# Last layer of a four-layer transformer: key and value projections folded into other weights

## The reference, cut to what matters

```python
nx = _layer_norm(x, ln_gamma, ln_beta)
q = nx @ Wq
k = prototype_bank @ Wk            # prototype_bank is the context
v = prototype_bank @ Wv
scores = einsum('bth,bph->btp', q, k) * H ** (-0.5)
weights = softmax(scores, axis=-1)
evidence = einsum('btp,bph->bth', weights, v)
combined = concatenate([nx, evidence, anchor], axis=-1)
router_probs = softmax(combined @ router_W + router_b, axis=-1)
h = silu(einsum('btc,ecr->bter', combined, e_w1) + e_b1)      # 3 experts, r = 256
expert_out = einsum('bter,erh->bteh', h, e_w2) + e_b2
routed = sum(expert_out * router_probs[..., None], axis=-2)
g = sigmoid(silu(combined @ gate_w1 + gate_b1) @ gate_w2 + gate_b2)
return x + g * (routed @ out_w + out_b)
```

## Time and profile before

| | |
|---|---|
| device time, median of 3 runs | 3569.41 us (3560.76 to 3570.86) |
| the profiled execution's own time | 3567.66 us |
| its span, first to last instruction | 3565.9 us |
| busy share of the span | PE 87%, DVE 77%, ACT 64%, PEld 58%, POOL 33% |
| last phase | from 3156.90 us to the end of the span |

### The profile page before, as it was taken

One profiled execution on the slowest core, in us unless ns is written; L12 is line 12 of the kernel. 1 busy time (PEld: TensorE's weight loads), 2 busy tenths in 40 slices (PEclk: granted clock), 3 DMA queues, 4 the chain that ended last, 5 costly groups with the idle time before them and its releaser, 6 DMA issues. The chain is left out here.

```text
span 3565.9 us, 94724 instructions
## 1 busy us (share of the span) xinstructions
PE 3088.2 (87%) x32127; PEld 2065.5 (58%) x32127; DVE 2757.3 (77%) x12477; ACT 2269.3 (64%) x5572; POOL 1172.1 (33%) x1374
## 2 busy tenths in 40 slices
PE   6999877777777769889999997889999998879999
PEld 3454434444444437656666665556666665558887
DVE  5888688999888978588887767868887775956665
ACT  2666567767667657557776665637776665646665
POOL 0000055665555656521122213531112211531221
PEclk9999988888778979999999998989999998979999
DMA  2111000000000000144444430034444441000000
GB/s 84 29 32 30 16 9 8 6 9 8 6 8 8 5 1 1 27 100 108 105 107 102 106 88 3 1 89 104 108 105 100 105 105 28 1 24 10 13 13 16
DMA packets 138900, 162.90 MB, mean 46 GB/s; under 512 B 41206, under 2 KB 88758, under 8 KB 138038
## 3 DMA queue, kind: packets, MB, share of 16 engines
q1 hardware_dynamic: 126262, 130.80, 14.5%
q0 software_dynamic: 12160, 26.04, 3.1%
HBM read 16.33 MB, written 4.19 MB: 6 GB/s over the span
## 5 line engine op out<-in xcount | busy, mean ns | idle before, releaser
L1367 ACT ACTIVATE attn_pT<-attn_t 128x512 f32<-128x512 f32 (+1 forms) x1024 | 556.3, 597 | 318.7 <-PE attn_t L1624 318.5
L1484 DVE TENSOR_REDUCE attn_mx<-attn_s 128x4 f32<-128x512 f32 (+1 forms) x1024 | 549.2, 578 | 136.6 <-PE attn_s L1609 135.4
L1609 PEld LDWEIGHTS attn_s<-packed_keys,packed_queries 32*128 32x128 f32 x4096 | 275.0, 188 | 162.8 <-DVE attn_mx L1484 96.9
L653 ACT ACTIVATE topk_prob<-topk_s,topk_nmx 128x77 f32<-128x77 f32 x1024 | 249.2, 327 | 182.3 <-DVE topk_work L832 156.1
L1282 POOL DMA_DIRECT2D packed_queries<-attn_om x256 | 143.0, 559 | 641.2 <-ACT attn_om L1360 637.3
L498 POOL TENSOR_SCALAR topk_mask<-topk_work 128x308 f32<-128x308 f32 x256 | 250.4, 978 | 314.4 <-DVE topk_work L837 313.3
L1609 PE MATMUL attn_s<-packed_keys,packed_queries 32*128 32x128 f32 (+1 forms) x4096 | 339.7, 286 | 15.4 <-DVE attn_mx L1484 9.1
L1649 PE MATMUL attn_o<-attn_pT,attn_vp 128*18 128x128 f32 (+1 forms) x8192 | 326.2, 277 | 0.0
L1027 PE MATMUL topk_t<-ident,topk_prob 128*77 128x128 f32 x1024 | 186.8, 313 | 138.0 <-POOL topk_prob L502 137.3
L1624 PE MATMUL attn_t<-packed_queries,packed_keys 32*128 32x128 f32 (+1 forms) x4096 | 300.1, 264 | 0.3 <-ACT attn_pT L1367 0.3
L1027 PEld LDWEIGHTS topk_t<-ident,topk_prob 128*77 128x77 f32 x1024 | 141.4, 172 | 242.8 <-issue 150.5
(11 more groups left out here) (316 smaller groups left out, 7859.0 us busy)
## 6 DMA issues: line engine op xcount, KB each, us to landing
packed_queries<-attn_qT SPq DMA_DIRECT2D x720, 64.0 KB, 2.2
packed_keys<-attn_kT SPq DMA_DIRECT2D x384, 64.0 KB, 2.1
packed_queries<-attn_om POOLq DMA_DIRECT2D x256, 64.0 KB, 2.3
packed_queries<-zero_rows SPq DMA_DIRECT2D x120, 128.0 KB, 2.7
packed_keys<-attn_kT SPq DMA_DIRECT2D x384, 39.0 KB, 2.2
kbd<-window_kT SPq DMA_DIRECT2D x512, 8.0 KB
kbd<-topk_kT SPq DMA_DIRECT2D x512, 4.8 KB
weights<-in_weights SPq DMA_DIRECT2D x1, 3267.0 KB, 13.1
```

The lines of the kernel that those rows point to most:

```text
L653: last = nc.scalar.activation(prob[:, u % 4, h * keys:(h + 1) * keys], s_ps[:, u % 2, h * keys:(h + 1) * keys], ACT.Exp, scale=SCALE, bias ...
L1367: nc.scalar.activation(pT[0:keys, c % 2, h, :], t_ps[0:keys, h, :], ACT.Exp, scale=SCALE).then_inc(s_exp, 1)
L1484: nc.vector.tensor_reduce(mx[:, (c // 2) % 2, 2 * k + h, :], sc, AX.X, ALU.max).then_inc(s_max, 1)
L1609: last = nc.tensor.matmul(s_ps[:, h, k * KW:(k + 1) * KW], r.qp[32 * j:32 * j + 32, buf, k, b * T:(b + 1) * T], r.kp[32 * j:32 * j + 32, b ...
```

## The change

Since scores = (nx Wq)(ctx Wk)^T = nx (Wq Wk^T) ctx^T, one matrix `wqk` = Wq Wk^T (made once on the chip) replaces `q3` in the query projection, and the scores read the context `r.ctxT` itself. Since evidence = weights (ctx Wv), the evidence is made from the context itself, loaded from HBM by SP into three buffers of `v`, and the rows of the experts', the gate's and the router's first weights that read the evidence are multiplied by Wv once on the chip (`folded()`). Wq, Wk and Wv are handed in transposed.

```diff
-        qT, kT, v = sb("qT", [C, GT]), sb("kT", [C, K4]), sb("v", [S, G, C])
+        qT, v = sb("qT", [C, GT]), sb("v", [S, 3, G, C])
...
+        def folded():
+
+            yield t_ps[:, :].rearrange("c (e n) -> c e n", e=2), [up_part(p, 1)[:, 0:2] for p in range(2)]
+            yield u_ps[:, 1:2, 2 * C:2 * C + RH], [up_part(p, 1)[:, 2:3] for p in range(2)]
+            yield g_ps[:, B * E:B * E + C], [w1s[:, p, E * 2 * RH + C:NU] for p in range(2)]
...
 @block.sync
+            def load_values(g):
+                sp.dma_start(v[:, g % 3], r.ctx_v[:, G * g:G * g + G, :]).then_inc(s_vin[g % 3], 16)
...
+            for g in range(3):
+                load_values(g)
             for g in range(NG):
                 p = g % 2
+                if there(g + 3):
+                    sp.wait_ge(s_eps, g + 1)
+                    load_values(g + 3)
                 sp.wait_ge(s_y, g + 1)
...
 @block.gpsimd, weights_low: only the halves that read nx (e1_first, first C columns of g1)
...
 @block.vector
-            def values_out(g):
-                dve.wait_ge(s_vps, g + 1)
-                nc.vector.tensor_copy(v[:, :, :], l_ps[0:S, :].rearrange("p (b c) -> p b c", b=G)
-                                      ).then_inc(s_v, 1)
...
 prepared():
                 nc.vector.tensor_copy(arb[:, :, :], by_batch(g_ps[:, 0:B * E], E)).then_inc(s_arb, 1)
+                for k, (product, parts) in enumerate(folded()):
+                    dve.wait_ge(s_fhi, k + 1)
+                    nc.vector.tensor_tensor(parts[1], product, parts[0].bitcast(F32), ALU.subtract).then_inc(s_flo, 1)
...
 @block.scalar
-            def keys_out(g):
-                act.wait_ge(s_kps, g + 1)
-                nc.scalar.copy(kT[:, :], l_ps[:, 0:K4]).then_inc(s_kT, 1)
...
 prepared():
+                for k, (product, parts) in enumerate(folded()):
+                    if k == 2:
+                        act.wait_ge(s_arb, 1)
+                        nc.scalar.copy(wr[:, :], g_ps[:, B * E + C:B * E + C + E]).then_inc(s_wr, 1)
+                    nc.scalar.copy(parts[0], product).then_inc(s_fhi, 1)
+
+            act.wait_ge(s_qkps, 1)
+            nc.scalar.copy(wqk[:, :], t_ps[:, 0:C]).then_inc(s_wqk, 1)
...
 @block.tensor
             def transpose_xn(g):
-                after(pe, s_v, g)
+                after(pe, s_qT, g)
...
-            def project_keys(g):
-                pe.wait_ge(s_nx, g + 1)
-                nc.tensor.matmul(l_ps[:, 0:K4], r.W("k3"), r.ctxT[:, G * g:G * g + G, :], start=True, stop=True
-                                 ).then_inc(s_kps, 1)
             def project_queries(g):
-                pe.wait_ge(s_kT, g + 1)
-                nc.tensor.matmul(l_ps[:, :], r.W("q3"), nx[:, g % NXB, :], start=True, stop=True).then_inc(s_qps, 1)
+                pe.wait_ge(s_nx, g + 1)
+                if g == 0:
+                    pe.wait_ge(s_wqk, 1)
+                nc.tensor.matmul(l_ps[:, :], wqk[:, :], nx[:, g % NXB, :], start=True, stop=True).then_inc(s_qps, 1)
-            def project_values(g):
-                pe.wait_ge(s_qT, g + 1)
-                for b in range(G):
-                    last = nc.tensor.matmul(l_ps[0:S, b * C:(b + 1) * C], r.ctxT[:, G * g + b, :], r.W("v3"),
-                                            start=True, stop=True)
-                last.then_inc(s_vps, 1)
...
             def scores(g):
                 after(pe, s_dif, g)
+                pe.wait_ge(s_qT, g + 1)
                 for b in range(G):
                     last = nc.tensor.matmul(s_ps[:, b * S:(b + 1) * S], qT[:, b * T:(b + 1) * T],
-                                            kT[:, b * S:(b + 1) * S], start=True, stop=True)
+                                            r.ctxT[:, G * g + b, :], start=True, stop=True)
...
 transpose_weights(0) also waits for s_flo 1; evidence(g) waits for s_vin[g % 3] in place of s_v and
 reads v[:, g % 3, b, :]; router(0) also waits for s_wr and s_flo 3 and reads wr; up number 0 for s_flo 3
...
             def prepare():
                 pe.wait_ge(s_w3, 16)
+                pe.wait_ge(s_wqk, 1)
+                for e in range(E):
+                    out = t_ps[:, e * RH:(e + 1) * RH] if e < 2 else u_ps[:, 1, 2 * C:2 * C + RH]
+                    nc.tensor.matmul(out, r.W("v3"), r.W("e1", (e * 3 + 1) * RH, RH), start=True, stop=True)
+                nc.tensor.matmul(g_ps[:, B * E:B * E + C], r.W("v3"), r.W("g1", C), start=True, stop=True)
+                nc.tensor.matmul(g_ps[:, B * E + C:B * E + C + E], r.W("v3"), r.W("rw", E, E), start=True, stop=True)
...
+            nc.tensor.matmul(t_ps[:, 0:C], r.W("q3"), r.W("k3"), start=True, stop=True).then_inc(s_qkps, 1)
             for i in range(-2, NG):
...
 the loop's calls of project_keys, project_values, keys_out and values_out go
```

More of the change, by code:

```diff
@@ L2074, in refine_phase @@
         w2ow = sb("w2ow", [C, 2 * E, C])
+        wqk, wr = sb("wqk", [C, C]), sb("wr", [C, E])
         b2bc, b2t = sb("b2bc", [C, E, C]), sb("b2t", [T, E, C])
@@ L2110, in refine_phase @@
         s_stats, s_mv, s_var, s_rstd, s_xn = sem("stats"), sem("mv"), sem("var"), sem("rstd"), sem("xn")
-        s_xT, s_nx, s_kps, s_kT, s_qps, s_qT, s_vps, s_v = (
-            sem(n) for n in ("xT", "nx", "kps", "kT", "qps", "qT", "vps", "v"))
+        s_xT, s_nx, s_qps, s_qT = (sem(n) for n in ("xT", "nx", "qps", "qT"))
+        s_vin = [sem("vin0"), sem("vin1"), sem("vin2")]
+        s_qkps, s_wqk, s_fhi, s_flo, s_wr = (sem(n) for n in ("qkps", "wqk", "fhi", "flo", "wr"))
         s_nxhi, s_nxlo, s_evhi, s_evlo = sem("nxhi"), sem("nxlo"), sem("evhi"), sem("evlo")
@@ L2133, in spread, with up_part @@
             return ap.rearrange("p (b a) -> p b a", a=1).broadcast_to([T, G, n])
-        e1_parts = r.W("e1", 0, E * 3 * RH).rearrange("c (e n) -> c e n", e=E)[:, :, 0:2 * RH]
+        e1_first = r.W("e1", 0, E * 3 * RH).rearrange("c (e n) -> c e n", e=E)[:, :, 0:RH]
+        def up_part(p, half):
+            return w1s[:, p, 0:E * 2 * RH].rearrange("c (e n) -> c e n", e=E)[:, :, half * RH:half * RH + RH]
+        def folded():
+            yield t_ps[:, :].rearrange("c (e n) -> c e n", e=2), [up_part(p, 1)[:, 0:2] for p in range(2)]
+            yield u_ps[:, 1:2, 2 * C:2 * C + RH], [up_part(p, 1)[:, 2:3] for p in range(2)]
+            yield g_ps[:, B * E:B * E + C], [w1s[:, p, E * 2 * RH + C:NU] for p in range(2)]
         @block.sync
         def _(sp):
+            def load_values(g):
+                sp.dma_start(v[:, g % 3], r.ctx_v[:, G * g:G * g + G, :]).then_inc(s_vin[g % 3], 16)
             sp.dma_start(r.w3[:, :], io["weights3"]).then_inc(s_w3, 16)
@@ L2179, in weights_low @@
                 pool.wait_ge(s_w1hi, 2)
[L2180 to L2184, removed]
+                nc.gpsimd.tensor_tensor(up_part(1, 0), e1_first, up_part(0, 0).bitcast(F32), ALU.subtract
+                                        ).then_inc(s_w1lo, 1)
+                nc.gpsimd.tensor_tensor(w1s[:, 1, E * 2 * RH:E * 2 * RH + C], r.W("g1", 0, C),
+                                        w1s[:, 0, E * 2 * RH:E * 2 * RH + C].bitcast(F32), ALU.subtract
+                                        ).then_inc(s_w1lo, 1)
             def output(g):
@@ L2348, in _ @@
                 if there(i + 2):
-                    values_out(i + 2)
                     difference(i + 2)
@@ L2419, in prepare @@
                 act.wait_ge(s_w3, 16)
[L2420 to L2423, removed]
+                nc.scalar.copy(up_part(0, 0), e1_first).then_inc(s_w1hi, 1)
+                nc.scalar.copy(w1s[:, 0, E * 2 * RH:E * 2 * RH + C], r.W("g1", 0, C)).then_inc(s_w1hi, 1)
             def prepared():
@@ L2448, in _ @@
                     hidden(i, 3)
-                if new:
-                    keys_out(i + 2)
                 if now:
@@ L2501, in transpose_weights @@
                 after(pe, s_ev, g)
+                if g == 0:
+                    pe.wait_ge(s_flo, 1)
                 pe.wait_ge(s_pn, g + 1)
@@ L2507, in evidence @@
             def evidence(g):
-                pe.wait_ge(s_v, g + 1)
+                pe.wait_ge(s_vin[g % 3], 16 * (g // 3) + 16)
                 pe.wait_ge(s_pT, g + 1)
                 for b in range(G):
-                    last = nc.tensor.matmul(t_ps[:, b * T:(b + 1) * T], v[:, b, :], pT[:, b * T:(b + 1) * T],
+                    last = nc.tensor.matmul(t_ps[:, b * T:(b + 1) * T], v[:, g % 3, b, :], pT[:, b * T:(b + 1) * T],
                                             start=True, stop=True)
@@ L2517, in router @@
                     pe.wait_ge(s_arb, 1)
+                    pe.wait_ge(s_wr, 1)
+                    pe.wait_ge(s_flo, 3)
                 after(pe, s_tg, g - 1)
@@ L2523, in router @@
                     last = nc.tensor.matmul(g_ps[:, b * E:(b + 1) * E], ev[:, g % 2, b * T:(b + 1) * T],
-                                            r.W("rw", E, E), start=False, stop=True)
+                                            wr[:, :], start=False, stop=True)
```

(6 more changed lines are left out.)

6 lines of the change are left out of this document (3 added, 3 removed).

## The result

| | before | after |
|---|---|---|
| device time, median | 3567.75 us (18 runs, 3558.65 to 3571.67) | 3542.99 us (18 runs, 3532.05 to 3562.26) |
| profiled execution | 3567.66 us | 3543.15 us |
| last phase, first statistics to the span's end | 3565.9 - 3156.95 = 408.95 us | 3541.4 - 3157.00 = 384.40 us |

The ratio is 0.9933, interval 0.992 to 0.9946: faster by 0.67%, 19 to 29 us of 3567.75. The two profiled executions reach the last phase within 0.05 us of each other, so the 24.5 us between them all lie in that phase, and its parts can be compared directly.

A forecast was written before the change was run, and what follows sets the result against it. The prediction took TensorE, busy throughout each loop step of the last phase, as the bound. It took 19.3 us (loop) plus 2.2 us (start), 21.5 us, off 3567.66 us, giving 3546 us, range 3537 to 3556.

The forecast's parts named there:

- The bound: Last phase's loop: TensorE is busy for all 22.93 us of a step, and the chain of waits never leaves it.
- The loop: Steps 0 to 13: removed key and value products save 1.38 us a step, 19.3 us in all (17.9 to 20.9).
- the 0.34 us behind the router: First matmul of `up` 4, now right behind the router: 0.34 us against 0.23, so the keys save 0.51 us.
- The 0.10 us at `up` 6: Step 14's slower `up` 6 start, put down to the late readout of `up` 4; not charged, kept as a bound.
- The other engines and the loads: Loop: DVE and ACT keep up with a 21.55 us step, and the new context loads stay hidden; cost 0.
- The cover: Context loads on SP: at least two whole steps, over 43 us, cover 2.3 us; without it, 2.3 us a load.
- Steps -2 and -1: Phase's start: 7.02 us saved, less 3.38 for folded products and 1.42 for subtractions; net 2.2 us (0 to 3.9).
- the best case: Phase's start: with the folded products at full clock, the net gain is 3.9 us.
- The sum: Whole kernel: 19.3 + 2.2 = 21.5 us saved (17.9 to 24.8), giving 3546 us; chance 0.80.
- part is given back at the start: Rival: the clock rises later at the phase's start, half clock for 7 us more of full-speed work; 3553 us, chance 0.12.
- The clock stays down for long: Rival: the loop's first 1.5 steps run at half clock, costing 32 us; 3578 us, chance 0.03.
- nothing moves: Rival: the removed products lay in TensorE time the loop waits anyway; only 2.2 us gained, 3565 us, chance 0.05.

The follow-up runs named there:

- discarded_keys: The changed kernel with the 308-column key product put back on TensorE in steps 0 to 13, result unread; ratio to the kernel before 0.9966.
- copies_twice: The kernel before with both copies that the change removes (keys on ACT, values on DVE) made twice; ratio to the kernel before 1.001.
- queries_early: The changed kernel with the query projection moved ahead of `up` 4, so `up` 4, 5 and 6 follow each other directly; ratio to the kernel before 0.9927.
- one_buffer: The changed kernel with one buffer for the loaded context in place of three, each load one group ahead; ratio to the kernel before 1.0276.
- folded_late: The changed kernel with the folded products moved behind the old ones in `prepare`; ratio to the kernel before 0.9948 in the first of two executions.
- values_only: The changed kernel with keys projected and copied again, so only the value fold is left; ratio to the kernel before 0.9976.
- keys_only: The kernel before with the key fold alone, values still projected and copied; ratio to the kernel before 0.996.
- warm_more: The changed kernel with unread products in TensorE's waits at the phase's start, after `prepare` and in steps -2 and -1; median 3535.50 us, ratio to the kernel before 0.9921.

## Why the prediction was right, and where it was off

- **The bound** held. TensorE fills the step before and after. That it was TensorE's place and nothing else is shown by discarded_keys (the product back, 0.51 us back) and copies_twice (copies doubled, nothing).
- **The loop**: 1.38 us a step predicted. The steps of 22.93 and 21.53 differ by 1.40, and what follows the start, 368.45 us before and 348.86 after, by 19.6 us against 19.3. A delay of 0.3 us in one step, described below, is already taken off the 19.6. Reading step 14 of the kernel before for the order that the change would make gave the 0.34 us behind the router exactly. The 0.10 us at `up` 6 were rightly not charged, and for the reason given: queries_early brings them back.
- **The other engines and the loads** cost nothing, as said. The cover was put somewhat too high: in the changed kernel a load of the loop is issued 38 to 39 us before its evidence (at 3331.44, for 3370.71), not over 43, because it stands behind the stores of the step before. The price of a lost cover, though, was put at the transfer's 2.3 us. one_buffer shows 6.5 us of stall, set by the place in SP's list, and 2.8 more by the clock.
- **Steps -2 and -1** were the term that was mis-sized: net 2.2 us (0 to 3.9) in the sum, 40.50 - 35.54 = 4.96 us measured, above the upper bound. The folded products cost 3.29 us for 3.38, DVE's subtractions 1.13 for 1.42. The error is the clock: I reckoned the folded products at half clock and left the rest of `prepare` at its old 6.70 us, and the best case doubled the speed of the folded products alone. In fact they ran at half clock and what stood behind them at full: 6.70 - 4.23 = 2.47 us. With it and the 0.29 and 0.09 us of the two prices, 2.2 becomes 5.05, near the 4.96.
- **The sum**: 21.5 predicted, 24.5 us between the profiled executions, 24.8 between the medians. 3546 against 3542.99, inside 3537 to 3556. The loop's 19.6 us were foreseen with their cause, 2.7 us at the start were not. The range is wide enough for that, since it holds the scatter of the three runs before.
- **The rivals**: "part is given back at the start" did not happen. It needed the last rise of the clock, the one behind the first `up` products, to come later. It came 2.4 us after the first matmul of `up` 0 (3194.95 against 3192.54), before the change 3.0 us after it (3200.42 against 3197.45). What I did not look at was the earlier rise inside `prepare`. There the folded products, up to 256 columns wide, come ahead of products of 64 columns, and the clock comes up earlier in all six profiles with this order (table under folded_late). values_only fits too. Its start of 39.74 us is longer than the changed kernel's because it still has the keys in it, 1.90 + 1.74 us, with 0.16 us for the queries behind them and 0.40 us in `prepare`. Together they are the 4.20 us between the two starts. "The clock stays down for long" and "nothing moves" did not happen.

## What to carry to other kernels

In a loop whose chain of waits never leaves one engine, an edit is worth the stream time that it takes from that engine's list, corrected for what the neighbours now uncover. A tail step that already has the new order shows that correction. Copies and loads hidden under such a loop are free to remove or add, but a load's cover is measured from where its issue stands in the queue, not from the transfer's own time. And where TensorE starts at half clock, price what stands behind an added dense product at both clocks too, not only the product.

## What the runs showed of the hardware that was not expected

- The phases ahead of the change, with the same instructions, ended between 3149.16 us (keys_only) and 3193.61 us (warm_more) in the profiles. That is far more than the change's whole gain. The granted clock goes with it: ahead of the last phase TensorE was at 0.50 for 417 us in keys_only, 451 us in the changed kernel and 544 us in warm_more (sums of the trace's clock record), and over all 14 profiles the phase begins later almost in the order of these sums. The whole times show it too: of the 34 runs of the kernel before that stood beside keys_only, the fastest, 3555.60 us, had a mean clock of 0.939 and the slowest, 3592.35 us, 0.922. Why equal instructions are granted so different a clock stays open. Differences of a few us must be read from the phase, not from the total.
- Stalls of TensorE of 6.5 us, in a loop otherwise at clock 1.00, brought the clock to 0.50, in each of the 14 steps that had one (one_buffer).
- Once in the loop of the changed kernel `down` stops for DVE, one of whose short operations starts 0.46 us late without a visible reason. The interval from gate product to gate product there (step 13 to 14, without a new group) is 19.75 to 19.79 us in every kernel with the value fold that kept its three buffers, and 19.48 to 19.51 in the kernel before, keys_only and copies_twice; the last has a single step of 23.20 us elsewhere. It keeps to a place in the program, and its cause stays open. The chain of waits of the changed kernel there:

```profile
3491.28 4.02 PE refine_e L2607 x36
3495.30 0.02 issue
3495.33 1.60 PE refine_e L2607 x12
```
